# Routing tables in two-byte elements with the choices innermost, token numbers first, and the first gather issued by the routing block

## The reference

```python
x = x + 0.5 * ffn(layernorm(x))
x = x + attention(layernorm(x))      # 32 heads of 16, ALiBi, causal
x = x + 0.5 * ffn(layernorm(x))

def ffn(x):                          # 8 experts, weights W_e [8, 512, 512]
    logits = x @ W_gate + b_gate
    _, top_idx = top_k(logits, 2)
    y_all = relu(einsum('bsd,edh->bseh', x, W_e) + b_e)
    return take_along_axis(y_all, top_idx[..., None], axis=2).mean(axis=2)
```

## Time and profile before

| | |
|---|---|
| median of 3 runs | 1060.15 us |
| profiled execution, its own time | 1064.33 us |
| its span, first to last instruction | 1062.6 us |
| mean granted TensorE clock | 0.924 of full speed |
| TensorE busy | 876.8 us, 83% |
| VectorE busy | 652.9 us, 61% |
| ScalarE busy | 446.5 us, 42% |
| GpSimd busy | 352.6 us, 33% |

### The profile page before, as it was taken

How to read it: one execution, slowest core, us unless ns; L and a number is a source line. 1 busy time by engine, 2 the same in 40 slices (tenths; PEclk the granted TensorE clock), 3 DMA queues, 4 the chain that set the end, 5 groups by cost and what they waited for, 6 DMA issues and landing times. The chain is left out here.

```text
span 1062.6 us, 20207 instructions
## 1 busy us (share of the span) xinstructions
PE 876.8 (83%) x6688; PEld 646.4 (61%) x6689; DVE 652.9 (61%) x1296; ACT 446.5 (42%) x818; POOL 352.6 (33%) x342
## 2 busy tenths in 40 slices
PE   2667699994698888858999999999859974699994
PEld 2556588873576776635555555555447763588873
DVE  6647244431988887757777777777427667344432
ACT  2332233331244343335777777777723430133321
POOL 4550577764022122120000000000024440577764
PEclk9997799997799999967999999999978995799998
DMA  8784578773244479664666666655148872378773
GB/s 247 268 276 119 165 142 153 140 134 50 82 152 150 154 194 207 179 203 103 145 134 140 132 138 133 140 132 112 33 140 264 292 246 99 85 142 154 135 136 52
DMA packets 112859, 162.08 MB, mean 153 GB/s; under 512 B 16864, under 2 KB 74336, under 8 KB 112512
## 3 DMA queue, kind: packets, MB, share of 16 engines
q1 hardware_dynamic: 94928, 123.85, 42.4%
q0 software_dynamic: 17856, 37.25, 19.1%
HBM read 97.44 MB, written 67.37 MB: 155 GB/s over the span
## 5 line engine op out<-in xcount | busy, mean ns | idle before, releaser
L827 DVE TENSOR_REDUCE att_part<-att_s_ps 128x2 f32<-128x1024 f32 (+2 forms) x160 | 195.4, 1225 | 61.4 <-PE att_s_ps L675 60.9
L789 ACT ACTIVATE att_prob<-att_st_ps 128x512 f32<-128x512 f32 x320 | 173.7, 595 | 78.7 <-PE att_st_ps L701 78.7
L143 PE MATMUL exp_z_ps<-ex_w_hi,exp_xT_hi 128*128 x312 | 131.7, 422 | 2.3 <-issue 1.0
L145 PE MATMUL exp_z_ps<-ex_w_hi,exp_xT_lo 128*128 x312 | 125.7, 403 | 0.0
L144 PE MATMUL exp_z_ps<-ex_w_lo,exp_xT_hi 128*128 x312 | 125.3, 402 | 0.0
L1470 DVE TENSOR_TENSOR exp_xT_lo<-exp_t_ps,exp_xT_hi 128x512 fp32r<-128x512 f32 x78 | 53.9, 692 | 106.7 <-ACT exp_xT_hi L1456 106.7
L1463 ACT ACTIVATE exp_y<-exp_y 128x512 f32<-128x512 f32 x72 | 45.5, 632 | 171.8 <-DVE exp_y L1482 171.8
L1099 POOL TENSOR_TENSOR ex_w_lo<-ex_bias,ex_w_hi 128x1024 fp32r<-128x1024 f32 x32 | 77.0, 2409 | 92.6 <-ACT ex_w_hi L1203 92.4
L1398 POOL DMA_INDIRECT exp_xg<-xn,ex_token_of x78 | 78.2, 1002 | 88.1 <-SPq L1370 60.4
L714 PE MATMUL att_pv_ps<-att_prob,att_v_sb 128*32 128x256 f32 (+2 forms) x1280 | 101.4, 391 | 1.8 <-ACT att_oT L794 1.8
L639 POOL CAST att_m_parts<-att_part 128x28 fp32r<-128x28 f32 x32 | 6.6, 208 | 271.3 <-DVE att_part L831 271.3
(11 more groups left out here) (199 smaller groups left out, 1713.4 us busy)
## 6 DMA issues: line engine op xcount, KB each, us to landing
ex_bias<-in_L_ffn_W_e SPq DMA_DIRECT2D x32, 512.0 KB, 6.8
...
```

The costliest lines, as they stand in the source:

```text
L143: nc.tensor.matmul(out, x_hi[:, s], w_hi(c), start=(c == 0), stop=False)
L145: last = nc.tensor.matmul(out, x_lo[:, s], w_hi(c), start=False, stop=(c == C - 1))
L789: nc.scalar.activation(prob[n % 2][:, col:col + 512], st_ps[(e + half) % 3][:, :], ACT.Exp).then_inc(exp_done, 1)
L827: nc.vector.tensor_reduce(out, src, X_AXIS, ALU.max, negate=True).then_inc(red_done, 1)
```

## The change

It has these parts. (1) The totals are no longer 16 matmuls of their own; they are treated as the ranks of a tile behind the last, in the 16 columns that follow the ranks, so each of the 15 rank matmuls is 16 columns wider and one matmul is added. (2) `at_tile` is laid out as three planes of 40 slot tiles by 32 choices, with the choices innermost. GpSimd writes the numbers 0 to 39 into plane 1 at the start (an iota of 1,280 elements); then three tensor_tensor operations, all in bf16, make the planes: compare, times `n_token_row`, times `n_token_tile`. The index matmul of choice n reads its 120 columns with a step of 32 elements. (3) `at_col` has room for all 32 choices, in buffers that are free by then, so VectorE doesn't wait for TensorE in it; `ids_done` is raised once. (4) `found` is copied right after the index matmuls. One operation writes `token_of` and raises `token_done`, the same sum is made again for `row_of`, then come `expert_of`, `row_of` and `before_of`. (5) GpSimd issues the first gather at the end of the routing block when `token_done` is raised. The identity, the six priming DMAs and the semaphores `gathered` and `added` belong to `Experts` now; the priming DMAs are issued and waited for in the routing block in front of the `w_lo` loop. In block 1 SyncE waits for the first gather to land before it issues the bias.

```diff
--- before.py
+++ after.py
@@ -866,8 +866,14 @@
-    def __init__(self, nc, ctx, prefix):
+    def __init__(self, nc, ctx, prefix, rows=None):
...
+        self.rows = m.sb("rows", [P, C, D]) if rows is None else rows
+        self.ident = m.sb("ident", [P, P])
+        self.prime = m.sb("prime", [1, ADD_RING * 16])
+        self.gathered = [m.sem(f"gathered{i}") for i in range(ADD_RING)]
+        self.added = [m.sem(f"added{i}") for i in range(ADD_RING)]
@@ -877,6 +883,11 @@
...
+    def gather(self, nc, xn_dram, s, xg):
+        nc.gpsimd.indirect_dma_start(out=xg, out_offset=None, in_=xn_dram[:, :],
+                                     in_offset=bass.IndirectOffsetOnAxis(ap=self.token_of[:, s:s + 1], axis=0)
+                                     ).then_inc(self.gathered[s % ADD_RING], 16)
@@ -907,9 +918,9 @@
...
-        ident = m.sb("ident", [P, P])
-        xn = [wo_turned[:, 2 * i:2 * i + 2, :] if proj else m.sb(f"xn{i}", [P, 2, D])[:, :, :] for i in range(2)]
+        ident = ex.ident
+        xn = [ex.rows[:, 2 * i:2 * i + 2, :] for i in range(2)]
@@ -929,16 +940,20 @@
...
-        COL_RING = 4
+        COLS = 8
+        at_col = [room.bitcast(BF16).rearrange("p (n c) -> p n c", n=COLS) for room in
+                  ([o[0][:, :], o[1][:, :], xT[0][:, :], xT[1][:, :]] if proj else [wo_turned[:, c, :] for c in range(C)])]
...
-        n_part = m.sb("n_part", [P, 1])
-        n_row = m.sb("n_row", [P, 2])
+        n_token_row = m.sb("n_token_row", [P, 2 * TILES], BF16)
+        n_none = m.sb("n_none", [P, 1])
@@ -967,13 +982,12 @@
...
-        slot_hi = m.sb("slot_hi", [P, 2 * TILES, 1], BF16)
+        slot_hi = m.sb("slot_hi", [P, 2 * TILES], BF16)
...
-        at_col = m.sb("at_col", [P, COL_RING, P], BF16)
-        at_tile = m.sb("at_tile", [P, 2 * TILES, 3, TAB], BF16)
+        at_tile = m.sb("at_tile", [P, 3, TAB, 2 * TILES], BF16)
...
-        past = m.sb("past", [1, TAB, E])
+        past = m.sb("past", [1, TAB, E])[:, :, :] if proj else xT[0][0:1, 0:TAB * E].rearrange("p (s e) -> p s e", e=E)
@@ -992,6 +1006,7 @@
...
+        token_done = m.sem("token_done")
@@ -1070,6 +1085,9 @@
...
+            if w_qkv is not None:
+                sp.wait_ge(ex.gathered[0], 16)
@@ -1082,22 +1100,36 @@
...
+            nc.gpsimd.iota(at_tile[:, 1, :, :], [[1, TAB], [0, 2 * TILES]], channel_multiplier=0, **small).then_inc(const_done, 1)
...
-            nc.gpsimd.iota(n_part[:, :], [[0, 1]], channel_multiplier=1, **small).then_inc(const_done, 1)
-            nc.gpsimd.iota(n_row[:, :], [[1, 2]], channel_multiplier=2, **small).then_inc(const_done, 1)
+            nc.gpsimd.iota(n_token_row[:, :], [[0, TILES // 2], [1, 2], [0, 2]], channel_multiplier=2, **small).then_inc(const_done, 1)
+            nc.gpsimd.iota(n_none[:, :], [[0, 1]], base=TOKENS, channel_multiplier=1,
+                           allow_small_or_imprecise_dtypes=True).then_inc(const_done, 1)
...
-            pool.wait_ge(const_done, 11)
+            pool.wait_ge(const_done, 12)
...
+            pool.wait_ge(ident_done, 1)
+            for r in range(ADD_RING):
+                nc.gpsimd.dma_start(ex.prime[0:1, r * 16:(r + 1) * 16], ident[0:1, 0:16]).then_inc(ex.added[r], 16)
+            for r in range(ADD_RING):
+                pool.wait_ge(ex.added[r], 16)
...
+            pool.wait_ge(tr_done, TILES)
+            for par in range(2):
+                pool.wait_ge(xn_stored[par], 16 * (PAIRS // 2))
+            pool.wait_ge(token_done, 1)
+            ex.gather(nc, xn_dram, 0, ex.rows[:, 0, :])
@@ -1160,16 +1192,14 @@
...
-            pe.wait_ge(const_done, 12)
+            pe.wait_ge(const_done, 13)
...
+            nc.tensor.matmul(total_ps, ones_bf[:, :], both[:, 0:2 * E], start=False, stop=False, skip_group_check=True)
...
-                last = nc.tensor.matmul(rank_ps[:, s * 2 * E:TE2], ones_bf[:, :], both[:, 0:TE2 - s * 2 * E], start=False,
-                                        stop=(s == TILES - 1), skip_group_check=True)
-            for s in range(TILES):
-                last = nc.tensor.matmul(total_ps, ones_bf[:, :], both[:, s * 2 * E:(s + 1) * 2 * E],
-                                        start=(s == 0), stop=(s == TILES - 1))
+                last = nc.tensor.matmul(route_ps[:, s * 2 * E:TE2 + 2 * E], ones_bf[:, :], both[:, 0:TE2 - (s - 1) * 2 * E],
+                                        start=False, stop=(s == TILES - 1), skip_group_check=True)
@@ -1177,8 +1207,9 @@
...
-                nc.tensor.matmul(id_ps, at_col[:, n % COL_RING, :], at_tile[:, n, :, :].rearrange("p a s -> p (a s)"),
-                                 start=(n == 0), stop=(n == 2 * TILES - 1)).then_inc(ids_done, 1)
+                last = nc.tensor.matmul(id_ps, at_col[n // COLS][:, n % COLS, :],
+                                        at_tile[:, :, :, n].rearrange("p a s -> p (a s)"), start=(n == 0), stop=(n == 2 * TILES - 1))
+            last.then_inc(ids_done, 1)
@@ -1279,7 +1310,7 @@
...
-            dve.wait_ge(const_done, 12)
+            dve.wait_ge(const_done, 13)
@@ -1324,27 +1355,33 @@
...
-            chain(nc.vector.tensor_copy(slot_hi[:, :, 0], slot_hi_i[:, :]))
+            chain(nc.vector.tensor_copy(slot_hi[:, :], slot_hi_i[:, :]))
...
-            every = [P, 2 * TILES, TAB]
-            chain(nc.vector.tensor_tensor(at_tile[:, :, 0, :], slot_hi[:, :, :].to_broadcast(every),
-                                          n_tile[:, :].rearrange("p (a s) -> p a s", a=1).to_broadcast(every), ALU.is_equal))
-            by_row = at_tile[:, :, :, :].rearrange("p (u k l) a s -> p u k l a s", k=2, l=2)
-            for k in range(2):
-                chain(nc.vector.tensor_scalar(by_row[:, :, k, :, 1, :], by_row[:, :, k, :, 0, :], n_row[:, k:k + 1], None, ALU.mult))
-            chain(nc.vector.tensor_tensor(at_tile[:, :, 2, :], at_tile[:, :, 0, :],
-                                          n_token_tile[:, :].rearrange("p (n a) -> p n a", a=1).to_broadcast(every), ALU.mult))
+            def by_choice(row, n):
+                return row.rearrange("p (a n) -> p a n", a=1).to_broadcast([P, n, row.shape[-1]])
+            chain(nc.vector.tensor_tensor(at_tile[:, 0, :, :], at_tile[:, 1, :, :], by_choice(slot_hi[:, :], TAB), ALU.is_equal))
+            chain(nc.vector.tensor_tensor(at_tile[:, 1, :, :], at_tile[:, 0, :, :], by_choice(n_token_row[:, :], TAB), ALU.mult))
+            chain(nc.vector.tensor_tensor(at_tile[:, 2, :, :], at_tile[:, 0, :, :], by_choice(n_token_tile[:, :], TAB), ALU.mult))
...
-                if n >= COL_RING:
-                    dve.wait_ge(ids_done, n - COL_RING + 1)
-                nc.vector.tensor_scalar(at_col[:, n % COL_RING, :], n_col[:, :], slot_lo[:, n:n + 1], None,
+                nc.vector.tensor_scalar(at_col[n // COLS][:, n % COLS, :], n_col[:, :], slot_lo[:, n:n + 1], None,
...
+            ids = id_ps.rearrange("p (a s) -> p a s", a=3)
+            dve.wait_ge(ids_done, 1)
+            chain(nc.vector.tensor_copy(found[:, :, :], ids))
+            nc.vector.scalar_tensor_tensor(ex.token_of[:, :], found[:, 2, :], float(P), found[:, 1, :],
+                                           ALU.mult, ALU.add).then_inc(token_done, 1)
+            chain(nc.vector.scalar_tensor_tensor(found[:, 1, :], found[:, 2, :], float(P), found[:, 1, :], ALU.mult, ALU.add))
...
+            chain(nc.vector.tensor_scalar(empty[:, :], found[:, 0, :], -1.0, 1.0, ALU.mult, ALU.add))
+            chain(nc.vector.scalar_tensor_tensor(ex.row_of[:, :], empty[:, :], n_none[:, :], found[:, 1, :], ALU.mult, ALU.add))
@@ -1354,15 +1391,6 @@
...
-            dve.wait_ge(ids_done, 2 * TILES)
-            chain(nc.vector.tensor_copy(found[:, :, :], id_ps.rearrange("p (a s) -> p a s", a=3)))
-            chain(nc.vector.scalar_tensor_tensor(found[:, 1, :], found[:, 2, :], float(P), found[:, 1, :], ALU.mult, ALU.add))
-            chain(nc.vector.tensor_copy(ex.token_of[:, :], found[:, 1, :]))
-            chain(nc.vector.tensor_scalar(empty[:, :], found[:, 0, :], -1.0, 1.0, ALU.mult, ALU.add))
-            chain(nc.vector.tensor_scalar(found[:, 2, :], empty[:, :], n_part[:, :], None, ALU.mult))
-            chain(nc.vector.scalar_tensor_tensor(found[:, 1, :], empty[:, :], float(TOKENS), found[:, 1, :], ALU.mult, ALU.add))
-            chain(nc.vector.tensor_tensor(ex.row_of[:, :], found[:, 1, :], found[:, 2, :], ALU.add))
@@ -1371,21 +1399,18 @@
...
-        ident = m.sb("ident", [P, P])
-        xg = [m.sb(f"xg{i}", [P, D]) for i in range(RING)]
+        ident = ex.ident
+        xg = [ex.rows[:, i, :] if i < C else m.sb(f"xg{i}", [P, D])[:, :] for i in range(RING)]
...
-        zeroed, ident_done = m.sem("zeroed"), m.sem("ident_done")
-        gathered = [m.sem(f"gathered{i}") for i in range(RING)]
-        added = [m.sem(f"added{i}") for i in range(RING)]
+        gathered, added = ex.gathered, ex.added
...
-        prime = m.sb("prime", [1, RING * 16])
@@ -1395,19 +1420,10 @@
...
```

(16 more changed lines are left out.)

## The result

The changed kernel takes 1066.82 us (median of 20 runs), the kernel before 1060.75 beside it (20 runs). The ratio, that of the means, is 1.0042, 95% interval 1.0025 to 1.0059, so **4.4 us slower** (2.7 to 6.3) where 5.1 us faster were forecast. Single runs scatter with a standard deviation of 2 to 3 us, so the total tells little of one step; the trace does. I read each step as a distance inside its own stage. The attention, which no edit touches, took 504.6 to 509.8 us in the first ten traces; this spread of 5 us is more than the edits here are worth, and the two profiled executions are equally long (spans of 1062.6 and 1062.7 us).

A forecast was written before the change was run, and what follows sets the result against it. TensorE, busy 83% of the span and full in the expert stage, stands still at both routing-to-expert hand-overs. Gains 3.7 + 2.2 less 0.8 make 5.1 us; 1060.15 - 5.1 = 1055.0 us, range 1051.8 to 1058.2.

The forecast's parts named there:

- the one on the priming: Expert block: removing six small DMAs, 3.02 + 2.03 us of GpSimd time with five gathers ahead, is worth nothing there.
- theory C: Expectation for 17 and 18: at a descriptor limit GpSimd clears part early, giving drains of about 4.2 and 4.32 us.
- Priming in block 1: Start of block 1: priming and iota delay the first w_lo; loss 0.8 us taken, bounds 0.1 to 2.4.
- Rank matmuls and tables: Routing blocks: rank matmuls gain 0.20 us a block; three table operations of 0.81 us gain 1.35 us a block.
- Index matmuls: Routing blocks: strided reads take up to 167 ns against VectorE's 163 ns pace; costed at nothing, upper end 0.1 us a block.
- a little over VectorE's pace: Rival, routing blocks: index matmuls take 200 ns, costing 1.2 us a block; total 1057.4 us, chance 0.12.
- Block 2: Second hand-over from routing to experts: first expert matmul at 910.3 instead of 913.96 us, gain 3.7 us.
- 0.7 less: Block 2 hand-over: the gain shrinks by 0.7 us if the routing block's end waits for gather 0.
- GpSimd's waking: End of routing block: GpSimd takes 0.9 us to wake and issue gather 0, bounds 0.3 to 0.4 and 1.27.
- Block 1: First hand-over from routing to experts: first expert matmul at 115.2 instead of 117.42 us, gain 2.2 us, up to 3.8.
- the 5.6 us for the DMAs beside the bias: Block 1 hand-over: gather 1 close behind the bias takes 5.6 us, lower bound 4.0; bias in by 113 us.
- the clock: Start of expert matmuls: half clock rises 2.7 us later in block 1, 4.9 in block 2; no change, ±1.1 us a block.

The follow-up runs named there:

- 3: Kernel before with only the six priming DMAs and their waits moved in front of the routing block's w_lo loop; ratio 1.0043.
- 6: Changed kernel with the six priming DMAs and their waits back in the expert block, behind gather 4; ratio 1.0025.
- 7: Changed kernel with the priming back in the expert block behind gather 4 and the tables as in the kernel before; ratio 1.0017.
- 14: Kernel before with its routing and expert blocks closed without GpSimd's drain; ratio 0.9919.
- 16: Kernel of 8 with its routing and expert blocks closed without GpSimd's drain; ratio 0.9847 to the kernel before.
- 8: Changed kernel with priming back in the expert block, tables by pairs of slot tiles, gathers 0 and 1 issued by the routing block; ratio 0.9974.
- 11: Kernel of 8 with two more priming DMAs in the expert block; ratio 1.0003 to the kernel before.
- 13: Kernel before with one more 64-byte GpSimd DMA issued in the routing block and waited for at the expert block's end; ratio 0.9997.
- 9: Kernel before with the six semaphores `added` declared outside the expert block; ratio 1.0013.
- 17: Kernel of 8 with two more small indirect gathers behind the priming in the expert block; ratio 1.0025 to the kernel before.
- 18: Kernel before with two more small indirect gathers behind the priming in the expert block; ratio 1.0071.
- 4: Changed kernel without SyncE's wait for gather 0 in front of the bias in block 1; ratio 1.0032 to the kernel before.
- 5: Changed kernel run again unaltered to see the spread; ratio 1.0035 to the kernel before.
- 15: Changed kernel with its routing and expert blocks closed without GpSimd's drain; ratio 0.9928 to the kernel before.
- 1: Changed kernel with GpSimd's waits for the priming DMAs moved behind the w_lo loop; ratio 1.0028 to the kernel before.
- experiment 2: Changed kernel with tables holding two neighbouring slot tiles side by side, so index matmuls read pairs of 4 bytes; ratio 1.0058 to the kernel before.

## Why the prediction was wrong

**The step that failed** is the one on the priming, "six small DMAs leave the expert block ... worth nothing there", and beside it what the text never looks at: the end of an expert block. The step costed the priming's removal only by the time GpSimd spends on it, 3.02 + 2.03 us with five gathers ahead. Moving it alone lengthened the drain from 4.15 to 6.43 us in both blocks (3); moving gather 0 and the identity and leaving the priming lengthened it to 6.85 (6, 7). The two drains of the changed kernel cost 4.4 us, and 14 to 16 show that such microseconds count in full. I had read the waits in front of TensorE, and at a block's end no engine is late for another: only one source line's drain tells it.

**What the drain depends on is partly open.** Each small DMA more in a block is 82 to 88 ns more on its drain: 6.353 us and 6.852 without and with the six priming DMAs (the changed kernel and 6), 6.767 and 6.931 with six and eight (8 and 11), and at the end of routing block 1 2.45, 2.54 and 2.95 us with none, one and six (before, 13, 3; 2.35 us of each is the wait for the last w_lo). The drain of most versions is 83 ns times the DMAs of the expert block. But the kernel before has 84 of them and 4.15 us, 50 times 83 ns, and so have 9 and 13; 17 and 18 lie off the line too. Every version is exact to a few ns in both blocks, so something in the program sets it and no chance. The place of the semaphores, the number of DMAs by itself, GpSimd's own computing, a DMA issued ahead and a limit on descriptors as theory C has it don't explain the two levels. What is left is the order of the DMAs and waits, in which the versions differ; that it is this order isn't shown, nor which order is the cheap one.

**Priming in block 1**: 0.8 taken, bounds 0.1 to 2.4; measured 2.45 from GpSimd's start to the logits. The upper bound had it, and the reason for staying far below it, that these packets are tiny, failed: the DMAs land late beside the first loads, 5.4 us behind their issue in the median. The same start also scatters: the logits come at 80.6 to 82.6 us in the five traces with the kernel before's start (before, 9, 13, 14, 18) and at 83.4 to 85.7 in the four with the changed kernel's (it, 4, 5, 15), and at 82.36 without the wait (1).

**Rank matmuls and tables** were right. The fifteen wide rank matmuls take 1.96 us and the totals are copied 0.04 after; three table operations of 0.82 to 0.83 us were forecast at 0.81. Two packed two-byte tensors run at (0.83 - 0.12)/1280 = 0.55 ns an element, with my 0.12 of fixed time. The Trainium skill, VectorE: DVE Perf Modes, perf-mode tier table, says twice the rate for this operation; the trace agrees, with 1.07 ns an element for the compare of before, (1.49 - 0.12)/1280.

**Index matmuls** were costed at nothing beside 163 ns; they are spaced 207, 1.4 us a block. This was the rival "a little over VectorE's pace" (200 ns, chance 0.12), and it was the case, though the forecast had cost it at nothing. The row I scaled by, a weight load with a step of 16 bytes at full clock, said 150 to 167 and was no measure of a moving operand at 64 bytes. The Trainium skill, SBUF — State Buffer, note on SBUF cachelines, spoke against the layout without a price; the trace agrees in direction, and experiment 2, with two neighbours on a line, removes the loss on TensorE.

**Block 2**: 3.7 forecast, 1.7 measured. The difference is 1.4 for the index matmuls and 0.6 for the block's end, which does wait for gather 0: the text has this as "0.7 less" and left it out of the sum. GpSimd's waking was right: 0.88 us from `token_of` to the gather, 0.9 taken.

**Block 1**: 2.2 forecast, 0.1 measured. The index matmuls are 1.4 later, GpSimd's and SyncE's chain 0.3 shorter than I had it, and gather 1 beside the bias takes 6.6 us from issue to its first use and the matmul stands 7.6 behind it, not 6.5. The failed term is the 5.6 us for the DMAs beside the bias, taken from gather 0 of before and used for gather 1 and for the bias itself: the bias landed 7.5 us behind its issue, and gather 1 was used 0.6 behind that. Holding the bias back until gather 0 is in cost 1.4 to 1.6 us (4).

By the rows: 2.45 - 1.7 - 0.1 + 4.4 = 5.1 us slower, 4.4 measured, with the expert stages left out. Behind the first expert matmul the clock rises (the matmuls' time falls from 0.63 to 0.39 us) after 2.3 us in block 1 and 4.9 in block 2, where it was 2.7 and 4.9, so it played next to no part there.
